# A recurrent decoder block on one core: weight preparation spread over three engines and layers, and the last batch's feed-forward rounds in three pairs of banks

## The reference

```python
for l in range(L):
    x = x + _slstm_layer(_ln(x, ln1_w[l]), conv_w[l], conv_b[l], wi[l], wf[l], wz[l], wo[l], rker[l], cell_b[l], gn_w[l])
    x = x + _ffn(_ln(x, ln2_w[l]), ff_up[l], ff_down[l])
return _ln(x, post_w)
```

```python
gate = jax.nn.silu(_bitlinear(x, w_gate))
up = _bitlinear(x, w_up)
return _bitlinear(gate * up, w_down)
```

## Time and profile before

| | before |
|---|---|
| median of 3 executions (lowest to highest) | 3622.69 us (3621.88 to 3623.40) |
| the profiled execution, its own time | 3622.36 us |
| its span in the profile | 3620.6 us |
| mean granted clock of TensorE | 0.988 |
| TensorE, VectorE, ScalarE, GpSimd busy | 97%, 93%, 84%, 64% |
| preparation, until the biases of step 0 start | 0 to 46.0 us |
| 279 recurrent steps | 47.1 to 2148 us |
| attention and feed-forward | to 3592.8 us |
| last batch's feed-forward and result | 3592.8 to 3620.6 us |

### The profile page before, as it was taken

The page is one execution under the profiler, slowest core; times in us unless marked ns, Lnnn a source line. Parts: engine busy times, 40 slices in busy tenths (PEclk is TensorE's granted clock), DMA queues, the critical chain, the costliest instruction groups (busy, mean ns, idle before and its releaser), DMA issues. The chain is left out here.

```text
span 3620.6 us, 168876 instructions
## 1 busy us (share of the span) xinstructions
PE 3509.0 (97%) x71457; PEld 2344.2 (65%) x71489; DVE 3363.6 (93%) x9400; ACT 3040.9 (84%) x6636; POOL 2307.3 (64%) x2515
## 2 busy tenths in 40 slices
PE   5999999999999999999999986999999999999997
PEld 3666666666666666666666653666666666666665
DVE  8999999999999999999999986999999999999987
ACT  4999999999999999999999983777777777777775
POOL 3777777777777777777777755555555555555552
PEclk9999999999999999999999998999999999999998
DMA  2001222110101000111000100000000000100000
GB/s 84 26 25 26 55 60 57 26 26 25 26 26 26 26 26 26 26 26 26 26 26 26 27 26 27 25 25 25 25 25 25 25 25 25 36 25 25 25 8 10
DMA packets 99981, 104.35 MB, mean 29 GB/s; under 512 B 17297, under 2 KB 95005, under 8 KB 98729
## 3 DMA queue, kind: packets, MB, share of 16 engines
q1 hardware_dynamic: 99224, 93.56, 9.0%
HBM read 48.52 MB, written 17.53 MB: 18 GB/s over the span
## 5 line engine op out<-in xcount | busy, mean ns | idle before, releaser
L572 POOL TENSOR_TENSOR conv_products<-normed_features,conv_taps_by_token 128x256 f32<-128x256 f32 (+1 forms) x837 | 756.5, 918 | 604.2 <-ACT normed_features L355 419.6
L299 PE MATMUL banks<-up_centred,after_cell_features 128*32 128x336 f32 x8928 | 683.7, 446 | 6.6 <-DVE after_cell L534 6.4
L787 POOL TENSOR_TENSOR exps_of_both_halves<-scores 128x256 f32<-128x256 f32 x512 | 404.0, 813 | 275.8 <-ACT scores L1067 273.3
L299 PEld LDWEIGHTS banks<-up_centred,after_cell_features 128*32 128x32 f32 x8928 | 300.2, 109 | 305.5 <-issue 245.2
L306 PE MATMUL banks<-down,hidden_features 112*32 112x256 f32 x6696 | 420.5, 383 | 0.9 <-issue 0.8
L1067 ACT ACTIVATE scores<-scores 128x512 f32<-128x512 f32 x512 | 302.4, 623 | 81.4 <-DVE scores L1218 81.4
L394 ACT ACT_TABLE_LOAD x279 | 358.0, 1283 | 5.0
L373 ACT ACT_TABLE_LOAD x279 | 358.0, 1283 | 5.0
L585 POOL TENSOR_TENSOR conv_partial_sums<-conv_products,conv_partial_sums 128x512 f32<-128x512 f32 x279 | 358.5, 1285 | 0.0
L1218 DVE SCALAR_TENSOR_TENSOR scores<-banks,score_top 128x512 f32<-128x512 f32 x512 | 317.3, 681 | 6.4 <-PE banks L893 2.9
L273 PE MATMUL banks<-recurrent_weights,h_features 64*32 64x256 f32 x8928 | 314.2, 380 | 0.0
(11 more groups left out here) (224 smaller groups left out, 9943.5 us busy)
## 6 DMA issues: line engine op xcount, KB each, us to landing
layer_inputs<-layer_outputs SPq DMA_DIRECT2D x279, 96.0 KB, 2.0
layer_inputs<-in_x SPq DMA_DIRECT2D x280, 32.0 KB, 1.8
x_scratch<-layer_outputs SPq DMA_DIRECT2D x279, 32.0 KB, 2.2
x_tokens<-in_x SPq DMA_DIRECT2D x32, 256.0 KB, 3.0
context_features<-in_ctx SPq DMA_DIRECT2D x32, 256.0 KB, 3.7
layers_out<-x_scratch SPq DMA_DIRECT2D x32, 256.0 KB, 2.8
out<-result SPq DMA_DIRECT2D x64, 128.0 KB, 1.8
up_centred<-in_ff_up SPq DMA_DIRECT2D x1, 2688.0 KB
```

What stands on the lines that cost most here:

```text
L299: mm = nc.tensor.matmul(bank[group(l), b, 0:UP], xmt[:, n, group(l)], up[:, l, n, at:at + UP], start=n == 0, stop=n == HALF - 1, skip_grou ...
L572: return nc.gpsimd.tensor_tensor(prod[:, i:i + n], xnt[:, j % NRING].rearrange("p n t -> p (n t)")[:, None, :].broadcast_to([P, n, HALF * ...
L787: nc.gpsimd.tensor_tensor(psum[:, i % RING, :], pr[:, i % RING, 0:S], pr[:, i % RING, S:2 * S], ALU.add).then_inc(halves_added, 1)
```

## The change

**Loads.** SyncE now issues the bias rows, then five small tensors (one semaphore), then `up` of layer 0, the gate weights, `up` of layers 1, 2 and 3, the recurrent weights and last `down`: 13 DMAs. TensorE waits for `down` in step 0.

**Preparation.** ScalarE takes the scaling of `up` layer by layer, that of the gate weights, both negations and the spread of the taps. GpSimd takes five memsets and the partial sums' start values. VectorE keeps the other memsets, makes the bias right after them, then `conv_w`, `centre`, `gnc`, and subtracts the means layer by layer, each as soon as TensorE has it. The memset of two banks is gone.

**End.** The last batch's rounds 0 to 3 use banks 6 and 7, 0 and 1, 2 and 3, 6 and 7; only round 3 waits, for the reads of round 0. ScalarE copies both token tiles ahead of `silu(f, 0)`. `h_max` follows `gated` round by round.

```diff
-            for dst, src in ((wg, a["gate_w"]), (rk, a["rker"]), (up, a["ff_up"]), (down, a["ff_down"]), (conv_w, a["conv_w"]), (conv_b, a["conv_b"]),
-                             (ln1, a["ln1"]), (ln2, a["ln2"]), (gnc, a["gn_w"]), (rows, a["bias"])):
-                sy.dma_start(dst[:], src).then_inc(w_loaded, DMA)
+            sy.dma_start(rows[:], a["bias"]).then_inc(rows_loaded, DMA)
+            for dst, src in ((ln2, a["ln2"]), (ln1, a["ln1"]), (conv_w, a["conv_w"]), (conv_b, a["conv_b"]), (gnc, a["gn_w"])):
+                sy.dma_start(dst[:], src).then_inc(small_loaded, DMA)
+            sy.dma_start(up[:, 0], a["ff_up"][:, 0]).then_inc(up_loaded[0], DMA)
+            sy.dma_start(wg[:], a["gate_w"]).then_inc(gates_loaded, DMA)
+            for l in range(1, LAYERS):
+                sy.dma_start(up[:, l], a["ff_up"][:, l]).then_inc(up_loaded[l], DMA)
+            sy.dma_start(rk[:], a["rker"]).then_inc(rk_loaded, DMA)
+            sy.dma_start(down[:], a["ff_down"]).then_inc(down_loaded, DMA)
...
-            pe.wait_ge(w_step, UP_SCALED)
+            pe.wait_ge(mean_made, 1)
             for l in range(LAYERS):
+                pe.wait_ge(up_scaled, HALF * (l + 1))
...
-            mm.then_inc(up_means, 1)
+                mm.then_inc(up_means, 1)
...
             nc.scalar.preload_act_table(ACT.Gelu)
+            act.wait_ge(small_loaded, SMALL * DMA)
+
+            def scale_up(l):
+                act.wait_ge(up_loaded[l], DMA)
+                for m in range(HALF):
+                    nc.scalar.activation(up[:, l, m, :], up[:, l, m, :], ACT.Identity, scale=ln2[:, l, m:m + 1]).then_inc(up_scaled, 1)
+
+            scale_up(0)
+            act.wait_ge(gates_loaded, DMA)
+            for l in range(LAYERS):
+                for m in range(HALF):
+                    w_ = wg[:, l, m, 2:4, :].rearrange("p g d -> p (g d)")
+                    nc.scalar.activation(w_, w_, ACT.Identity, scale=ln1[:, l, m:m + 1]).then_inc(gates_made, 1)
+            f_ = wg[:].rearrange("p l h g d -> p (l h) g d")[:, :, 1, :]
+            nc.scalar.activation(f_, f_, ACT.Copy, scale=-1.0).then_inc(gates_made, 1)
+            for l in range(1, LAYERS):
+                scale_up(l)
+            act.wait_ge(conv_made, 1)
...
+            for buf, val in ((xr, 0.0), (xm, 0.0), (h, 0.0), (half_r, 0.0), (prod, 0.0)):
+                nc.gpsimd.memset(buf[:], val).then_inc(zeroed, 1)
+            pool.wait_ge(small_loaded, SMALL * DMA)
+            for turn_ in range(2):
+                for k in range(TAPS + 1):
+                    b_ = conv_b[:].rearrange("p l n -> p n l")
+                    nc.gpsimd.tensor_scalar(part[:, turn_, k].rearrange("p (n l b) -> p n l b", n=HALF, l=LAYERS),
+                                            b_[:, :, :, None].broadcast_to([P, HALF, LAYERS, B]), 0.5, None, ALU.mult).then_inc(parts_made, 1)
...
+    def round_banks(j, r):
+
+        if j < B - 1 or r % 3 == 0:
+            return FFB, FFB + 1
+        return 2 * r - 2, 2 * r - 1
...
+                if j == B - 1 and r == 1:
+                    pe.wait_ge(clip_done, AHEADS * B)
+                    pe.wait_ge(ot_done, QUADS * B)
                 for m, read in enumerate((gate_done, h_done)):
-                    if r > 0:
+                    if j < B - 1 and r > 0:
                         pe.wait_ge(read, ROUNDS * j + r)
+                    elif r == 3:
+                        pe.wait_ge(read, ROUNDS * j + 1)
...
-            x_features(f, [0])
-            silu(f, 0)
-            x_features(f, [1])
-            for r in range(1, ROUNDS):
+            x_features(f, [0, 1])
+            for r in range(ROUNDS):
                 silu(f, r)
...
             for r in range(ROUNDS):
                 gated(f, r)
-            for r in range(ROUNDS):
                 h_max(f, r)
```

More of the change, by code:

```diff
@@ L32 @@
 ROW_SCALE = 16.0
-UP_SCALED = 39
 EPS = 1e-5
@@ L340, in _ @@
                 pe.wait_ge(grown, j + 1)
+                if j == 0:
+                    pe.wait_ge(down_loaded, DMA)
                 feed_down().then_inc(down_done, 1)
@@ L360, in _ @@
             nc.scalar.preload_act_table(ACT.Gelu)
+            act.wait_ge(small_loaded, SMALL * DMA)
[14 more added lines that the diff above has]
+            act.wait_ge(conv_made, 1)
+            for k in range(TAPS):
+                w_ = conv_w[:, :, :, TAPS - 1 - k].rearrange("p l n -> p n l")
+                nc.scalar.activation(taps[:, k], w_[:, :, :, None].broadcast_to([P, HALF, LAYERS, B]), ACT.Copy).then_inc(gates_made, 1)
+            act.wait_ge(rk_loaded, DMA)
+            f_ = rk[:].rearrange("p l h g d -> p (l h) g d")[:, :, 1, :]
+            nc.scalar.activation(f_, f_, ACT.Copy, scale=-1.0).then_inc(gates_made, 1)
             act.wait_ge(first_gates, 1)
@@ L409, in _ @@
                 n += 2
[L410 to L419, removed]
@@ L420, in _ @@
-            dve.wait_ge(const_made, 4)
[L421 to L444, removed]
@@ L465, in _ @@
             nc.vector.tensor_scalar(pick16[0:3 * LAYERS], pick[:], 1.0 / ROW_SCALE, None, ALU.mult).then_inc(bias_made, 1)
-            dve.wait_ge(up_means, 1)
+            for r in (0, 64):
+                nc.vector.tensor_scalar(centre[r:r + DH, :], ident[r:r + DH, r:r + DH], -1.0 / DH, None, ALU.add).then_inc(w_step, 1)
+            dve.wait_ge(small_loaded, SMALL * DMA)
+            nc.vector.scalar_tensor_tensor(out=conv_w[:], in0=conv_w[:], scalar=0.5, in1=ln1[:][:, :, :, None].broadcast_to(
+                [P, LAYERS, HALF, TAPS]), op0=ALU.mult, op1=ALU.mult).then_inc(conv_made, 1)
+            n += 2
+            dve.wait_ge(w_step, n)
+            nc.vector.tensor_tensor(gnc[:].rearrange("p l n d -> p (l n) d"), gnc[:].rearrange("p l n d -> p (l n) d"),
+                                    centre[:, None, :].broadcast_to([P, LAYERS * HALF, DH]), ALU.mult).then_inc(w_step, 1)
+            n += 1
+            dve.wait_ge(zeroed, 2)
+            nc.vector.bn_stats(stat2[:], xm[:, 0]).then_inc(w_step, 1)
+            n += 1
             for l in range(LAYERS):
+                dve.wait_ge(up_means, l + 1)
                 for m in range(HALF):
@@ L472, in _ @@
             dve.wait_ge(w_step, n)
[L473 to L476, removed]
             dve.wait_ge(bias_made, 10)
+            dve.wait_ge(parts_made, 2 * (TAPS + 1))
+            dve.wait_ge(gates_made, SCALED)
+            dve.wait_ge(cleared, 9)
             dve.sem_inc(w_ready, 1)
@@ L1083, in silu @@
                 act.wait_ge(gu_ready, ROUNDS * j + r + 1)
-                nc.scalar.activation(gate[:, tt, c * 512:(c + 1) * 512], bank[:, FFB, :], ACT.Silu,
+                nc.scalar.activation(gate[:, tt, c * 512:(c + 1) * 512], bank[:, round_banks(j, r)[0], :], ACT.Silu,
                                      scale=deq[:, tt, 0:1]).then_inc(gate_done, 1)
```

26 lines of the change are left out of this document (18 added, 8 removed).

## The result

The changed kernel takes 3594.56 us (median of 4 runs, 3592.03 to 3598.31) against 3622.28 us for the kernel before (4 runs beside it, 3620.08 to 3623.4): a ratio of 0.9925, 95% interval 0.9913 to 0.9938. It is faster, by 27.7 us. Its profiled execution took 3594.75, with a span of 3593.0.

A forecast was written before the change was run, and what follows sets the result against it. TensorE is busy 97% of the span, so only the two ends can gain: preparation 22.15 + step 0 1.0 + last batch 4.5 = 27.65 us, from 3622.36 to 3594.7, the median 0.33 higher at 3595.0; range 3591 to 3602.

The forecast's parts named there:

- the preparation: Before the first bias matmul: it starts at about 23.85 instead of 46.0 us, a gain of 22.15.
- the last batch: Feed-forward at the end: rounds no longer wait and `h_max` follows `gated`, a gain of 4.5 us, bounds 3.9 and 6.6.
- step 0 with its lead-in: First step: TensorE idle 1.8 us ahead of it, not 10, gives 1.0 us, bounds 0 and 2.25.
- the prediction's estimate from that page: Loads: at the page's 341 GB/s layer 3 would land near 17.8 and the sum be 1.1 us longer.
- Rival A: Preparation: TensorE's means run at the low rate, gain smaller by 1.3 to 5.3 us, 3597.3 to 3601.3; chance 0.15.
- The term of GpSimd: Preparation: five memsets 3.6 us and ten partial sums at about 0.35 each, 3.5 us, done near 11, hidden by VectorE.
- The 12 us of cover: Preparation: GpSimd's work would be on the path only if it took over 12 us more.
- Rival B: Preparation: VectorE's bias and GpSimd's partial sums block each other, 3598.4 or 3602.2 us; chance 0.14.
- C: Rival on the loads: they don't land in order, preparation gains only 10.5 us, 3606.7 in all; chance 0.07.
- D: Rival on the steps: they lengthen, 0.1 us more per step cancels the gain, slower than before; chance 0.02.
- E: Rival on the last batch: later silu 0 or round 1's wait costs what the rounds save, 3599.5 us; chance 0.03.

The follow-up runs named there:

- changed_again: The changed kernel itself, with no edit, measured once more: 3595.59 us (5 runs), ratio 0.9925 to the kernel before.
- sums_after_bias: The changed kernel, but GpSimd's ten partial sums start only when VectorE's bias operations are done: 3598.83 us (one run).
- keep_busy_end: The changed kernel plus 40 unread matmuls, 20 ahead of the last batch's first transposes and 20 behind its last round: 3592.46 us (one run).
- busy_throughout: The changed kernel plus unread matmuls around the means, in step 0 and in the last batch: 3591.9 us (5 runs), ratio to before 0.9918.
- keep_busy_front: The changed kernel plus 18 unread matmuls, 8 between last mean and first bias matmul, 10 in step 0's pause: 3595.13 us (one run).
- all_loads_first: The changed kernel, but ScalarE waits for all large loads before it scales layer 0: 3611.82 us (one run).
- end_only: The kernel before with only the new last batch, its preparation as before: 3617.51 us (10 runs), ratio 0.9986.
- scale_on_vector: The changed kernel with all of ScalarE's preparation given back to VectorE, loads and GpSimd's share as changed: 3604.62 us (one run).

## Why the prediction was right

Predicted 3595.0, measured 3594.56; 27.65 us of gain against 27.60 between the profiled executions. The closeness is partly luck: the preparation gave 22.42 (22.15 predicted), the last batch 5.61 (4.5), step 0 with its lead-in 0.0 (1.0), the other 278 steps, where no instruction changed, 0.38, and the middle -0.80. The profiled execution is also the quickest of its kind at the front: with the same front, the first bias matmul came at 23.59, 23.61, 24.25, 24.39 and 25.49 in five profiles.

- **Loads.** Predicted landings 8.3 (layer 0), 10.7 (gate weights), 17.9 (recurrent weights), 22.5 (`down`); measured 7.8, 10.2, 6.31 + 11.5 = 17.8, 22.6. From 6.0 to 15.0 us, where the four transfers of 672 KB and the gate weights land, the rate was 405 to 444 GB/s; before, with larger ones, it was 410 to 470. The Trainium skill, page "DMA: Bandwidth & Descriptors", section "Rules for kernel authors", wants at least 1 MiB per DMA, and the prediction's estimate from that page was a sum 1.1 us longer. Queued behind each other, as here, these transfers paid no such price. `bias_moved` was predicted for 22.9; in changed_again and sums_after_bias it landed only near 24.2 and 24.9 and was the last wait.
- **ScalarE.** Two scalings of a layer 1.60 (predicted 1.5), gate weights 10.24 to 13.20, layers 1 to 3 done at 17.68 (18.2): right.
- **TensorE.** Layer 0 took 4.32, not 3.5: all its pairs ran at the low pace, not only six, and that pace is 0.54 to 0.56. The gap behind it was therefore 0.87, not 1.8. Layers 1 to 3 ran at the full pace, 14.75 to 21.80 (predicted 15.2 to 22.0). Rival A did not happen here, but its slow pace did in keep_busy_end, and by a fall of the granted clock in busy_throughout; it is not refuted.
- **VectorE and GpSimd.** The last subtraction ended at 23.45 (predicted 23.6), the first bias matmul came at 23.59 (23.85). The term of GpSimd was badly mis-sized: ten partial sums at an estimated 0.35 each, 12.33 in all instead of 3.5; even without the hold it is 8.3 (VectorE had taken 2.11 for them before). The 12 us of cover that the prediction had named held. Rival B's mechanism is shown by sums_after_bias, but it cost VectorE 0.6 us, not the 3.5 or more of the rival, and that was hidden behind TensorE's means. The Trainium skill, page "SBUF — State Buffer", section "Who interferes with whom", says that a VectorE operation with two SBUF inputs contends with a GpSimd one that reads SBUF. The trace agrees on GpSimd's side (sums of up to 2.08 us beside such operations, 0.84 at the quickest); on VectorE's side the two-input operations did not get longer.
- **Step 0, the step that failed.** The prediction gave it 1.0 us from a full clock, "TensorE would now be idle 1.8 us ahead of it, not 10". It lost 0.43 instead. TensorE's rest of 2.5 us is inside step 0, from 24.59 to 27.06, and the clock fell there: the pause ahead of the step was looked at, the one in it not. With fillers in both pauses (keep_busy_front) the clock stays up and the step takes 9.09. That is 1.1 less than in the changed kernel and 0.7 less than before. The other 1.6 over a mean step may be an empty pipeline, as the prediction said; no run tests it. The 16 bias matmuls did run at full clock (0.63 us instead of 1.05), which brought the first ScalarE operation another 0.4 nearer and balanced the loss; with the 0.7 it would have made the 1.0 good.
- **Last batch.** Predicted 4.5, bounds 3.9 and 6.6; measured 5.61. The rounds and `h_max` gave 11.94 - 7.10 = 4.84. The prediction had round 0 to the last `h_max` at 7.6: silu 0 was late by 0.53 (0.6 predicted), and rounds 1, 2 and 3 were ready 1.96, 3.52 and 4.38 behind round 0 (2.1, 3.8, 5.55 predicted), since the clock rose at the end of round 2 (0.62 in the window of 3576 to 3577). The 16 output matmuls also profited from a clock that rose during them: from the second tile's transposes of `hidden` to the last `x_plus_ff` 3.75 instead of 4.49. That both kinds of matmul can run quicker had been a bound, and came true in part. How much depends on when the clock rises: in changed_again it rose and fell again ahead of the output matmuls, which took 3.56, and the stretch was 22.59.
- **Other rivals.** C is refuted by the landings above and by all_loads_first; its price was 2.4 us too small, since behind ScalarE's last scaling TensorE would have had two layers left and not one. D is refuted by the steps: (2117.68 - 24.29)/278 = 7.53, as before, E by end_only, 5.6 us.

What stays open is when TensorE's pace doubles: 3 us into the means in the kernel before, 9 us into them in keep_busy_end, where the pause behind the first layer didn't change it. The granted clock is recorded as 1.00 throughout both.

## What to carry to other kernels

A long preparation is a pipeline like any other: one semaphore per part of the load, the parts in the order of their use, and the work spread by which engine is idle at that time gave 22 us here, though the new engine was slower at it (0.80 us per scaling against 0.49). Where two engines alternate on a pair of buffers at the drained end of a kernel, look for buffers whose owners have finished. Before a gain by the clock is counted, look for TensorE's pauses inside the stretch as well as ahead of it, and put a filler only where it does not lengthen the pause behind it. A small transfer that the next stage needs should not be queued behind a large one that it doesn't.

## What the runs showed of the hardware that was not expected

- The matmul pace can be half the full one with a granted clock recorded as 1.00: pairs 0.56 apart at the start of every preparation without fillers ahead of it, until 18.29 us in keep_busy_end, with the clock at 1.00 in all windows there. The pace of the pairs, not the clock column, tells the rate at the start of a kernel.
- The granted clock can fall while TensorE works: after a rest of 2.75 us (busy_throughout) it was still 1.00 when the matmuls came back at 14.74, and 0.59 and 0.50 in the windows of 16 to 17 and 17 to 18, both 100% busy. In step 0 it fell at the end of a rest of 2.5 us, and stayed low to 33 to 34 us.
- A GpSimd operation on 128x256 floats with one input took 0.83 us when VectorE's bias operations were done, about twice ScalarE's 0.42, and 1.23 on average beside them. Ten of them had taken VectorE 2.11 us in all (L443 of the kernel before). GpSimd's memset of 128x1536 took 1.37, about VectorE's 1.34.
- The hold between the two engines is not only one of two-input operations: in scale_on_vector, sums beside VectorE's one-input scalings took up to 1.25 us, and those scalings 0.69 each (median) instead of the 0.57 of before.
